# A causal convolution's taps taken from the matrix engine's folded weights to evictions on ScalarE and VectorE, in a two-layer Mamba, attention and expert kernel on one Trainium2 core

## The reference, cut to what matters

```python
xz = x @ Win                      # 128 -> 2 * 256
xi, z = jnp.split(xz, 2, axis=-1)
xi = jax.nn.silu(_causal_dwconv(xi, convw, convb))   # per channel, 4 taps
xdbc = xi @ Wx                    # 256 -> 8 + 16 + 16
dt_in = xdbc[..., :DT_RANK]
Bm = xdbc[..., DT_RANK:DT_RANK + D_STATE]
Cm = xdbc[..., DT_RANK + D_STATE:]
dt = jax.nn.softplus(dt_in @ Wdt + bdt)              # 8 -> 256
A = -jnp.exp(Alog)
y = _selective_scan(xi, dt, A, Bm, Cm, Dp)           # h = exp(dt A) h + dt u B
return y * jax.nn.silu(z) @ Wout
```

## Time and profile before

| | us |
|---|---|
| median of 3 executions | 2081.15 (2073.28 to 2085.22) |
| the profiled execution | 2084.03 |
| its span, first to last instruction | 2081.9 |
| PE busy | 1770.7 (85% of the span) |
| DVE busy | 1582.0 (76%) |
| ACT busy | 1093.9 (53%) |
| POOL busy | 798.9 (38%) |
| mean granted PE clock | 0.919 of full speed |

### The profile page before, as it was taken

One profiled execution on the slowest core, in us unless ns is written; L12 is line 12 of the kernel. 1 busy time (PEld: TensorE's weight loads), 2 busy tenths in 40 slices (PEclk: granted clock), 3 DMA queues, 4 the chain that ended last, 5 costly groups with the idle time before them and its releaser, 6 DMA issues.

```text
span 2081.9 us, 27272 instructions
## 1 busy us (share of the span) xinstructions
PE 1770.7 (85%) x8504; PEld 818.7 (39%) x8544; DVE 1582.0 (76%) x2148; ACT 1093.9 (53%) x1494; POOL 798.9 (38%) x632
## 2 busy tenths in 40 slices
PE   4543488989988999989998999989998999989888
PEld 1220133443343434443343434443444435434545
DVE  1888888779886898879986898869987899641404
ACT  2424376357734775357734676367734675334122
POOL 0345544244543454234543445235533446220101
PEclk9665698999999999999999999999999999999989
DMA  7889998458845786458745786558745786400000
GB/s 211 223 208 222 225 218 206 112 147 193 195 105 147 168 203 167 119 136 196 194 106 144 168 204 165 123 137 194 194 116 136 167 204 184 107 11 0 6 1 5
DMA packets 108200, 310.54 MB, mean 149 GB/s; under 512 B 16000, under 2 KB 32272, under 8 KB 108048
## 3 DMA queue, kind: packets, MB, share of 16 engines
q1 hardware_dynamic: 93840, 280.36, 56.1%
q10 hardware_dynamic: 14208, 28.32, 4.2%
HBM read 288.71 MB, written 19.92 MB: 148 GB/s over the span
## 4 chain that ended last, share of the span: by engine, by line
PE 49%; DVE 18%; issue 14%; ACT 8%; POOL 5%; DMA 2%; DVEq 1%; ACTq 0%; POOLq 0%
PE ps_pair L700 11%; PE ps_pair L856 8%; PE ps_pair L797 8%; DVE sb_hst L1278 6%; PE ps_pair L785 6%; PE ps_pair L650 4%; PE ps_pair L876 3%; POOL sb_hc L1540 3%; ACT sb_mix L1100 2%; PE ps_y L632 2%; DMA sb_ring<-spread_dram 2%; DVE ps_in L1270 2%; DVE sb_dd L1256 2%; DVE sb_dd L1252 2%; PE ps_pair L800 2%
## 5 line engine op out<-in xcount | busy, mean ns | idle before, releaser
L1540 POOL TENSOR_TENSOR sb_hc<-sb_hst,sb_crep 128x512 f32<-128x512 f32 x512 | 658.8, 1296 | 891.4 <-DVE sb_hst L1278 566.0
L1278 DVE TENSOR_TENSOR_SCAN sb_hst<-sb_ring,ps_in 128x512 f32<-128x512 f32 x512 | 621.4, 1214 | 74.6 <-POOL sb_hc L1540 50.6
L952 ACT ACTIVATE sb_ring<-sb_ring,sb_A 128x512 f32<-128x512 f32 x512 | 344.1, 712 | 163.3 <-DMA sb_ring<-spread_dram 105.3
L1270 DVE TENSOR_TENSOR ps_in<-sb_ring,ps_brow 128x512 f32<-128x512 f32 x512 | 354.6, 693 | 21.5 <-DMA sb_ring<-spread_dram 4.1
L856 PE MATMUL ps_pair<-sb_mix,sb_ew 128*128 128x512 f32 x512 | 270.6, 668 | 6.1 <-DVE sb_g L1357 3.3
L921 ACT ACT_TABLE_LOAD x196 | 251.5, 1283 | 14.3 <-DVE sb_xd L1318 5.6
L632 PE MATMUL ps_y<-sb_hc,sb_const 128*32 128x512 f32 x1024 | 153.1, 673 | 70.7 <-POOL sb_hc L1540 58.4
L797 PE MATMUL ps_pair<-sb_g,sb_h 128*128 128x512 f32 x320 | 161.4, 627 | 26.8 <-ACT sb_mix L1100 12.0
L785 PE MATMUL ps_pair<-sb_h,sb_g 128*128 128x512 f32 (+3 forms) x512 | 164.6, 453 | 5.1 <-DVE sb_nmax L1409 4.3
L856 PEld LDWEIGHTS ps_pair<-sb_mix,sb_ew 128*128 128x128 f32 x512 | 103.0, 212 | 154.9 <-issue 115.0
L876 PEld LDWEIGHTS ps_pair<-sb_ew,sb_eh 128*128 128x128 f32 x1024 | 120.0, 192 | 23.3 <-issue 22.5
(11 more groups left out here) (218 smaller groups left out, 2147.0 us busy)
## 6 DMA issues: line engine op xcount, KB each, us to landing
sb_ring<-spread_dram SPq DMA_DIRECT2D x512, 512.0 KB, 5.7
spread_dram<-sb_dd ACTq DMA_DIRECT2D x32, 512.0 KB, 2.9
sb_brep<-cut_dram ACTq DMA_DIRECT2D x16, 256.0 KB, 3.7
sb_crep<-cut_dram ACTq DMA_DIRECT2D x16, 256.0 KB, 4.0
sb_xtok<-in_L_attn_x_dram SPq DMA_DIRECT2D x8, 256.0 KB, 5.0
sb_ew<-in_L_ffn_w_dram SPq DMA_DIRECT2D x2, 1024.0 KB, 8.4
out_dram<-sb_yy ACTq DMA_DIRECT2D x8, 256.0 KB, 2.3
sb_h<-in_L_ffn_h_w_dram SPq DMA_DIRECT2D x1, 1024.0 KB, 7.3
```

What stands on the lines that cost most here:

```text
L952: act.activation(ring[:, n % RING, 0, :], ring[:, n % RING, 0, :], ACT.Exp, scale=A[d][:, g:g + 1]).then_inc(sem["dA"], 1)
L1270: dve.tensor_tensor(ps_in[n % 2][:], ring[:, n % RING, 1, :], ps_brow[:], ALU.mult).then_inc(sem["dbu"], 1)
L1278: dve.tensor_tensor_scan(hst[:, HST_SLOT[n], :], ring[:, n % RING, 0, :], ps_in[n % 2][:], 0.0, ALU.mult, ALU.add).then_inc(sem["scan"], 1)
L1540: pool.tensor_tensor(hc[:, n % 6, :], hst[:, HST_SLOT[n], :], crep[n // NU][:], ALU.mult).then_inc(sem["hc"], 1)
```

## The change

1. **xi**: `winx` holds Win itself, and PE makes one product per half instead of four (`[moving]`, where `moving` is `xT` or its reversed view). The last tap is an ACT eviction with a scale and the bias per channel into `u` (Identity, semaphore `tap`). DVE adds the three other taps to `u` out of the PSUM bank, three instructions for each half, six for a direction (L1307, semaphore `conv`). ACT then takes SiLU of `u` in place, in the piece that already does SiLU of z. The bank is free after DVE's last tap (`conv`), no longer after ACT's eviction.
2. **The time step**: the bias bdt becomes a row of Wdt, against a row of ones in `xd`, so that the product brings v + b; the product reads 41 rows for 8. ACT makes |v|, the exponential, a square (the series by its vertex), Relu(small - exponential) as the mask, and the logarithm. POOL's step is gone. DVE has four large instructions for six. The bank of dtp is free when dt is done (`dt`), no longer after max(v + b, 0) (`rpos`).
3. **Start**: no folding of taps; the taps come as a small transfer; GpSimd clears `wdt` first (`w_zero`) and SP waits for that before its loads.
4. **Orders**: a head has 9 and 8 steps for 11 and 10, GpSimd has no heads, and all strings are new.

```diff
+THIRD = 3.0 ** -0.5
...
-HEAD = [["xT"], ["xi00", "xi01"], ["z00", "z01"], ["x0"], [], ["dtp0"], [], [], ["dtp1"], [], [],
-        ["xi10", "xi11"], ["z10", "z11"], ["x1"], [], ["dtp2"], [], [], ["dtp3"], [], []]
+HEAD = [["xT"], ["xi00", "xi01"], ["z00", "z01"], ["x0"], [], ["dtp0"], [], ["dtp1"], [],
+        ["xi10", "xi11"], ["z10", "z11"], ["x1"], [], ["dtp2"], [], ["dtp3"], []]
...
     if name[:2] == "xi":
-        return "u", half
+        return "conv", 6 * int(name[2]) + int(name[3]) + 5
     if name[:3] == "dtp":
-        return "rpos", int(name[3]) + 1
+        return "dt", int(name[3]) + 1
...
+                sp.wait_ge(w_zero, 1)
...
-                    product(f"xi{d}{h}", [winx[d][:, k, h * P:(h + 1) * P] for k in range(KC)],
-                            [shifted(k) for k in range(KC)])
+                    product(f"xi{d}{h}", [winx[d][:, h * P:(h + 1) * P]], [moving])
...
-                rows = slice(64 * d, 64 * d + R)
+                rows = slice(64 * d, 64 * d + R + 2 * S + 1)
...
             def dt_step(row, hf, made):
...
-                act.wait_ge(sem["dt"], row("dt", hf))
+                act.wait_ge(sem["du"], row("du", hf))
                 act.wait_ge(sem["kept"], row("kept", 16 * hf))
-                act.activation(dd[:, 0, :], made()[:], ACT.Abs, bias=cols[d][:, 1, h:h + 1]
-                               ).then_inc(sem["absd"], 1)
+                act.activation(dd[:, 0, :], made()[:], ACT.Abs).then_inc(sem["absd"], 1)
...
-                act.activation(tser, texp[:], ACT.Identity, scale=1.0 / 3.0, bias=mhalf[:, 0:1]
+                act.activation(tser, texp[:], ACT.Square, scale=THIRD, bias=vertex[:, 0:1]
                                ).then_inc(sem["third"], 1)
+                act.activation(tsel[:], texp[:], ACT.Relu, scale=-1.0, bias=small[:, 0:1]).then_inc(sem["small"], 1)
...
                 for h in range(NH):
-                    act.activation(u[d][:, h, :], full(f"xi{d}{h}")[:], ACT.Silu, bias=cols[d][:, 0, h:h + 1]
-                                   ).then_inc(sem["u"], 1)
+                    act.activation(u[d][:, h, :], full(f"xi{d}{h}")[:], ACT.Identity, scale=taps[d][:, h, KC - 1:KC],
+                                   bias=cols[d][:, 0, h:h + 1]).then_inc(sem["tap"], 1)
...
+                for h in range(NH):
+                    act.wait_ge(sem["conv"], row("conv", 6 * d + 5 + h))
+                    act.activation(u[d][:, h, :], u[d][:, h, :], ACT.Silu).then_inc(sem["u"], 1)
...
-            for d in range(2):
-                taps = rawconv[d].rearrange("p (c k) -> p c k", k=KC)
-                for k in range(KC):
-                    ins = dve.tensor_tensor(winx[d][:, k, :], rawin[d], taps[:, :, k], ALU.mult)
...
-                if k == 0:
-                    dve.wait_ge(sem["absd"], row("absd", hf + 1))
-                    dve.tensor_scalar(tpos[:], made[:], cols[d][:, 1, h:h + 1], 0.0,
-                                      ALU.add, ALU.max).then_inc(sem["rpos"], 1)
-                elif k == 1:
-                    dve.wait_ge(sem["series"], row("series", hf + 1))
-                    link(1, dve.scalar_tensor_tensor(tser, tser, 1.0, texp[:], ALU.add, ALU.mult))
-                    dve.wait_ge(sem["logd"], row("logd", hf + 1))
-                    link(2, dve.tensor_scalar(tsel, texp[:], SMALL, None, ALU.is_le))
-                    dve.memset(tick[:], 0.0)
-                    link(3, dve.copy_predicated(dd[:, 0, :], tsel, tser))
-                    dve.tensor_tensor(dd[:, 0, :], dd[:, 0, :], tpos[:], ALU.add).then_inc(sem["dt"], 1)
...
+                dve.wait_ge(sem["third"], row("third", hf + 1))
+                dve.scalar_tensor_tensor(tser, tser, 0.8125, texp[:], ALU.add, ALU.mult).then_inc(sem["series"], 1)
...
+                dve.copy_predicated(dd[:, 0, :], tsel[:].bitcast(U32), tser).then_inc(sem["log1p"], 1)
+                dve.wait_ge(sem["log1p"], row("log1p", hf + 1))
+                dve.scalar_tensor_tensor(dd[:, 0, :], made[:], 0.0, dd[:, 0, :], ALU.max, ALU.add).then_inc(sem["dt"], 1)
+                dve.wait_ge(sem["dt"], row("dt", hf + 1))
+                dve.tensor_tensor(dd[:, 1, :], dd[:, 0, :], u[d][:, h, :], ALU.mult).then_inc(sem["du"], 1)
...
+                for s in range(1, KC):
+                    for h in range(NH):
+                        o, done = u[d][:, h, s:T], 6 * d + 2 * (s - 1) + h
...
+                        dve.scalar_tensor_tensor(o, bank[tab[f"xi{d}{h}"][0][0]][:, 0:T - s], taps[d][:, h, KC - 1 - s:KC - s], o,
+                                                 ALU.mult, ALU.add).then_inc(sem["conv"], 1)
...
-            def dt_step(row, hf):
-                pool.wait_ge(sem["third"], row("third", hf + 1))
-                pool.tensor_tensor(tser, tser, texp[:], ALU.mult).then_inc(sem["series"], 1)
```

135 lines of the change are left out of this document (61 added, 74 removed).

## The result

The changed kernel takes 1984.28 us (median of 4, 1983.65 to 1990.75), the kernel before on the same chip 2082.07 (2073.28 to 2085.22). The ratio is 0.954 [0.951, 0.958], some 95 us less; I had forecast 2036. The profiled execution took 1983.65, its span is 1981.8.

What follows compares the result with a forecast made beforehand. PE and DVE were taken as nearly full before the attention, a chain as setting the attention. From 2084.0, start -8, second section -3, loop -30 and last section -3.5 gave 2039.5, a median of 2036 us; range 2000 to 2068.

Steps and rivals of the forecast that it cites:

- the first stretch: The part of a loop turn before the attention (experts, heads, feed-forward parts), 148.5 us; forecast to take 131 us.
- POOL loses four instructions of 1.276, 5.1 us, hidden: Time step in the loop: POOL's multiplication goes, 5.1 us less POOL work in a turn, counted as hidden.
- Net: 1.9 us more on DVE in a turn: DVE in a loop turn: 8.2 us removed, taps add 8.9 and the last product 1.2; range 0.7 to 1.9.
- I take 10 us of idle for the new mixture: 131 us: Loop turn before the attention: 121 us of PE work plus 10 us of PE idle makes 131 us.
- Attention: 13.5 idle, 94: Attention in a loop turn: 81 us of PE work plus 13.5 us idle, 94 us in all, from 82.2.
- a stall of the third scores: Attention's third round: scores start 8.3 to 9.3 us later behind a time step; 6 us of idle added per turn.
- The ends: Sections outside the loop's turns: first section 0, second -3 us, last section -3.5, flush 0.
- Start: Before the first section: no folding (4.25 us), fewer xi products and shorter first time steps, together -8 us.
- The signs: Whole kernel: PE's busy time falls about 90 us to 1680, DVE's rises 5 to 20, POOL's falls 41.
- The taps pay in full: Rival: PE's 11.3 us come out of every loop turn; 2009 us, a median of 2006; chance 0.18.
- Slower: Rival: ACT's queue in the attention's rounds stalls about 16 us a turn; 2089 to 2100 us; chance 0.07.
- nothing out of the loop: Rival: DVE's taps and a stall of 12 take PE's gain; a median of 2068 us; chance 0.13.

## Why the prediction was wrong

The direction was right, and so was the outline of a turn, in which the attention grows (by 14.1 us, to 96.3 where I had 94) and the first stretch shrinks (by 27.4). The size was not, by more than a factor of two. The steps, the one that failed most first:

- **"POOL loses four instructions of 1.276, 5.1 us, hidden": the step that failed most.** The term was put at nothing, and no reason was given. Taken away alone POOL's step is worth 26 us in the old orders, and it had kept PE's relief from getting through (10 us alone, 34 on top of it). POOL's instruction was indeed covered; what it did to DVE was not: 14 us of waits in front of the step and 20 us in its own instructions, and by the norm behind it PE lost 11 us in the loop. In the first stretch DVE stood at 134.5 of 148.5 us; I had called that nearly full, and took it only as a reason for PE's idle time to stay.
- **"Net: 1.9 us more on DVE in a turn".** It fell by 6.0. The taps (8.9 put, 8.4 to 8.9 measured) were right. The time step lost 2.67 us, four times 10.7 in a batch (12.6 in a turn of the loop, where POOL is busier), where I had 8.2 less 1.2 for the last product. I had left L1252 out: I knew from the earlier trace rows that its neighbours are long with POOL at work, and looked for no such row of it. That last product I put at 1.0, since it takes the place of L1257; its mean is 0.728, near the lower bound of 0.69. The Trainium skill (SBUF — State Buffer, Who interferes with whom) would make it wait for POOL. The trace agrees, but seldom: the six of 32 that start while a read-out of POOL has 0.33 us to go take 0.88 to 0.89 us, the others 0.69, 0.04 more on average.
- **"I take 10 us of idle for the new mixture: 131 us" with 4.3 of rest.** From norm to norm, rest included, that is 135; it was 126.1, with 7.1 of idle, and this stretch has most of what the turn gave beyond the forecast. (131, 94 and 4.3 make 229.3, and the rest of a turn was 4.8; the 229.5 is off by 0.3 at most.) **"Attention: 13.5 idle, 94".** 12.3 and 96.3, right as numbers; PE has 84 us of work there where I had 81. But its reason, a stall of the third scores, shows only 11.1 us of waits in the whole run, not 5 in each turn. That the number came out is in part luck.
- **PE.** A turn lost 14.3 us of busy time and not 11.3. The clock, 0.98 for 0.96, can account for the rest: 2% of 202 us is 4. So it is over the whole run: 110.2 us less, 90.6 of them taken away, and the mean clock at 0.930 for 0.919, 1.2% of 1680 us or 20. Why it was granted more no run isolates.
- **The ends.** The last section gave 16.4 where I had 3.5, the second 7.4 for 3, the first 4.3 for 0, the flush 1.7 for 0: 23 us that I missed by saying that the orders there were almost the same. Behind the last turn it is the new orders: 464.6 us before, 464.5 without POOL's step, 460.6 with PE's relief too, 461.1 and 464.0 with all the work in the old orders, against 446.5 (446.8 to 453.0 with work put back).
- **Start**, the only term too large: -2.8 for -8. The folding gave its 4.25, but the taps' bank and z's evictions, which I had not put on the chain, took it back. One of my own signs of being wrong showed here: PE waits 1.7 us at product x for SiLU of `u`.
- **The signs.** PE's busy time is 1660.5 us (1680 put), DVE's fell by 34.9 instead of rising by 5 to 20, POOL's fell by 44.1 (41 put).
- **The rivals.** "The taps pay in full" (2006) had nearly the right turn (224 for 222.0), and for PE the right reason. What no rival held was that DVE could get lighter. "Slower" and "nothing out of the loop" both rest on DVE or the rounds being loaded more; the rounds were, by 14.1 us, but the first stretch gave almost twice that.

Open is how the new orders' worth splits: against the same work in the old ones they are worth up to 70 us, 33 of which may be the merged instruction, and half of it lies outside the loop. The runs show that they are fitted closely: what is added to either engine costs 78 to 90% of its length, what is moved costs 4 to 22 us (4 is inside the noise), and 24 us is all that came of taking 95 away. They don't show which wait it is that remains. No run that keeps the whole computation was faster than the changed kernel.
